# Attention scores as three products of split queries and keys, the parts made per head on ScalarE and GpSimd

## The reference, cut to what matters

```python
q = (x @ wq + bq).reshape(N, H, Dh) * Dh ** (-0.5)      # H = 4 heads, Dh = 128
k = (x @ wk + bk).reshape(N, H, Dh)
v = (x @ wv + bv).reshape(N, H, Dh)
scores = jnp.einsum('ehd,ehd->eh', q[src], k[dst])
smax = jax.ops.segment_max(scores, src, num_segments=N)
ex = jnp.exp(scores - smax[src])
denom = jax.ops.segment_sum(ex, src, num_segments=N)
attn = ex / denom[src]
out = jax.ops.segment_sum(attn[:, :, None] * v[dst], src, num_segments=N)
return out.reshape(N, D) @ wo + bo
```

## Time and profile before

| what | value |
|---|---|
| median of 3 runs | 1652.49 us (1652.28 to 1654.07) |
| the profiled execution, own time | 1657.46 us |
| its span | 1655.8 us |
| TensorE busy | 95% |
| VectorE, ScalarE, GpSimd busy | 71%, 66%, 41% |
| mean granted TensorE clock | 0.989 |
| attention stages of the four blocks | about 234 to 297, 395 to 459, 556 to 620, 715 to 777 us |

### The profile page before, as it was taken

One profiled execution on the slowest core, in us unless ns is written; L12 is line 12 of the kernel. 1 busy time (PEld: TensorE's weight loads), 2 busy tenths in 40 slices (PEclk: granted clock), 3 DMA queues, 4 the chain that ended last, 5 costly groups with the idle time before them and its releaser, 6 DMA issues. The chain is left out here.

```text
span 1655.8 us, 24985 instructions
## 1 busy us (share of the span) xinstructions
PE 1568.6 (95%) x8530; PEld 1222.1 (74%) x8530; DVE 1181.7 (71%) x1900; ACT 1099.5 (66%) x1530; POOL 672.1 (41%) x494
## 2 busy tenths in 40 slices
PE   5789899999999999999999999999999999999987
PEld 5765586878688768877854777777777777777874
DVE  8977645555565546464623499888888888888967
ACT  9841545544554456444530599999999999999962
POOL 3410200120012001200302788888888888888500
PEclk9999899999999999999999999999999999999989
DMA  3001220022012200211106867777777777777710
GB/s 105 0 19 66 90 83 26 20 63 84 26 33 83 77 1 33 83 33 69 49 1 221 162 140 151 149 139 156 141 153 147 149 148 146 150 139 155 163 38 32
DMA packets 107046, 153.94 MB, mean 93 GB/s; under 512 B 42042, under 2 KB 47034, under 8 KB 106466
## 3 DMA queue, kind: packets, MB, share of 16 engines
q0 software_dynamic: 72832, 87.84, 27.3%
q1 hardware_dynamic: 34146, 65.21, 12.2%
HBM read 141.02 MB, written 11.73 MB: 92 GB/s over the span
## 5 line engine op out<-in xcount | busy, mean ns | idle before, releaser
L1752 POOL DMA_INDIRECT edge_gathered<-dst_table,edge_index x158 | 262.2, 1660 | 58.6 <-issue 54.0
L223 PE MATMUL edge_z2p<-edge_w_hi,edge_h_hi 128*128 128x512 f32 x628 | 256.7, 409 | 1.7 <-DVE edge_late L2067 1.7
L223 PE MATMUL edge_z2p<-edge_w_hi,edge_h_lo 128*128 128x512 f32 x628 | 248.7, 396 | 0.0
L223 PE MATMUL edge_z2p<-edge_w_lo,edge_h_hi 128*128 128x512 f32 x628 | 248.5, 396 | 0.0
L1721 POOL DMA_INDIRECT edge_gathered<-src_table,edge_index x158 | 186.3, 1179 | 85.4 <-issue 34.6
L961 POOL TENSOR_TENSOR h<-h,tr_row_b 128x512 f32<-128x512 f32 x40 | 59.1, 1514 | 264.7 <-ACT C L1196 264.4
L950 POOL TENSOR_TENSOR tr_cw<-w_c,tr_cw 32x1024 fp32r<-32x1024 f32 x7 | 16.6, 2375 | 363.7 <-ACT tr_cw L1156 363.7
L223 PEld LDWEIGHTS edge_z2p<-edge_w_hi,edge_h_hi 128*128 128x128 f32 x628 | 118.0, 188 | 54.8 <-issue 29.8
L223 PEld LDWEIGHTS edge_z2p<-edge_w_hi,edge_h_lo 128*128 128x128 f32 x628 | 118.2, 188 | 28.6
L2067 DVE TENSOR_TENSOR edge_late<-edge_z2p,w_c 128x1024 f32<-128x1024 f32 x79 | 96.7, 1224 | 57.3 <-PE edge_z2p L223 55.9
L223 PEld LDWEIGHTS edge_z2p<-edge_w_lo,edge_h_hi 128*128 128x128 f32 x628 | 118.3, 188 | 24.6
(11 more groups left out here) (362 smaller groups left out, 4004.7 us busy)
## 6 DMA issues: line engine op xcount, KB each, us to landing
w_c<-in_attr_T SPq DMA_DIRECT2D x78, 128.0 KB
agg<-edge_sum_rows POOLq DMA_DIRECT2D x36, 128.0 KB
w_a<-in_wv SPq DMA_DIRECT2D x4, 1024.0 KB, 5.4
w_b<-in_wq SPq DMA_DIRECT2D x4, 1024.0 KB, 5.4
w_a<-in_wk SPq DMA_DIRECT2D x4, 1024.0 KB, 7.9
w_b<-in_wo SPq DMA_DIRECT2D x4, 1024.0 KB, 7.0
w_a<-in_m SPq DMA_DIRECT2D x4, 1024.0 KB, 5.3
w_b<-in_m SPq DMA_DIRECT2D x4, 1024.0 KB, 5.4
```

What stands on the lines that cost most here:

```text
L223: mm = pe.matmul(out, a, b, start=(n == 0), stop=(n == last))
L1752: pool.indirect_dma_start(out=from_rows[ring][:, j, :].bitcast(F32), out_offset=None, in_=k.dst_table, in_offset=bass.IndirectOffsetOnAxis ...
```

## The change

The scores become three products like the others. For each head ScalarE copies k (`k_high`) and q (`q_high`) into fp32r high parts, GpSimd subtracts to make the low parts (`low_rows`), and TensorE waits for both (`qk_split`) before a head's first score product. Two k buffers alternate: head 0 and 2 in the first 640 columns of the flattened `hid` buffers, head 1 and 3 in the last chunk of `yT`. The q parts go by node tiles of 128 columns into a ring of 7 slots behind the first k buffer; where five tiles wrap around the ring's end, the copy and the subtraction come in two runs (heads 1 and 2). `k_high(0)` and `q_high(0)` stand ahead of the loop over n, `k_high(h+1)` at n = 5h+1 and `q_high(h+1)` at n = 5h+3 ahead of that n's exponential.

```diff
--- before.py
+++ after.py
@@ -750,6 +750,21 @@
         r, y = k.h, k.C
         yT_hi, yT_lo = sb("yT_hi", [P, KF, NP], F32R), sb("yT_lo", [P, KF, NP], F32R)
         hid_hi, hid_lo = sb("hid_hi", [P, KF, 3 * P], F32R), sb("hid_lo", [P, KF, 3 * P], F32R)
+        flat_hi, flat_lo = (t[:, :, :].rearrange("p c n -> p (c n)") for t in (hid_hi, hid_lo))
+        k_parts = [(flat_hi[:, 0:NP], flat_lo[:, 0:NP]), (yT_hi[:, KF - 1, :], yT_lo[:, KF - 1, :])]
+        Q_RING = 7
+        q_parts = [(flat_hi[:, NP + a * P:NP + (a + 1) * P], flat_lo[:, NP + a * P:NP + (a + 1) * P]) for a in range(Q_RING)]
+
+        def q_runs(h):
+
+            runs, i = [], 0
+            while i < NT:
+                slot = (h * NT + i) % Q_RING
+                n = min(NT - i, Q_RING - slot)
+                runs.append((i, slot, n))
+                i += n
+            return runs
+
         qT, kT, v = sb("qT", [P, KF, NP]), sb("kT", [P, KF, NP]), sb("v", [P, NT, D])
         probs_more = sb("probs_more", [P, NP])
         scores, probs = [k.hT[:, a, :] for a in range(2)], [k.hT[:, 2, :], k.hT[:, 3, :], probs_more[:, :]]
@@ -772,6 +787,7 @@
             sem(n) for n in ("vec", "sca", "var_ready", "rstd_ready", "h_ready", "exp_ready", "probs_ready",
                              "y_ready", "bias_added", "x_joined"))
         y_high, o_high, hidden_split = sem("y_high"), sem("o_high"), sem("hidden_split")
+        qk_high, qk_split = sem("qk_high"), sem("qk_split")
         cb_scaled, cw_high, cw_ready = sem("cb_scaled"), sem("cw_high"), sem("cw_ready")
         gcn_h_ready, edge_h_ready = sem("gcn_h_ready"), sem("edge_h_ready")
         plan = Plan(sem("product_ready"), {"vec": sem("taken_vec"), "sca": sem("taken_sca"), "low": sem("taken_low"),
@@ -951,6 +967,17 @@
                                        ALU.subtract).then_inc(cw_ready, 1)
                     pool.wait_ge(cw_ready, b * 2 + (s + 1))
 
+                def low_rows(b, h):
+
+                    pool.wait_ge(qk_high, (b * HEADS + h) * 2 + 1)
+                    hi, lo = k_parts[h % 2]
+                    pool.tensor_tensor(lo, kT[:, h, :], hi.bitcast(F32), ALU.subtract).then_inc(qk_split, 1)
+                    pool.wait_ge(qk_high, (b * HEADS + h) * 2 + 2)
+                    for i, slot, n in q_runs(h):
+                        at = slice(NP + slot * P, NP + (slot + n) * P)
+                        ins = pool.tensor_tensor(flat_lo[:, at], qT[:, h, i * P:(i + n) * P], flat_hi[:, at].bitcast(F32), ALU.subtract)
+                    ins.then_inc(qk_split, 1)
+
                 pool.wait_ge(cw_ready, 1)
                 cut(0, 1)
                 for b in range(BLOCKS):
@@ -959,9 +986,15 @@
                         pool.wait_ge(y_ready, of_norm(b, s, NT - 1))
                         for i in range(NT):
                             pool.tensor_tensor(r[:, i, :], r[:, i, :], row_b[:, :], ALU.add).then_inc(bias_added, 1)
+                        if s == 0:
+                            for h in range(HEADS - 1):
+                                low_rows(b, h)
+                            pool.wait_ge(qk_split, (b * HEADS + HEADS - 2) * 2 + 2)
                         if b < LAST:
                             pool.wait_ge(bias_added, of_norm(b, s, NT - 1))
                             cut(b + 1, s)
+                        if s == 0:
+                            low_rows(b, HEADS - 1)
                 for i in range(NT):
                     pool.wait_ge(bias_added, of_norm(LAST, 1, i))
                     pool.tensor_tensor(k.x[:, i, :], k.x[:, i, :], r[:, i, :], ALU.add).then_inc(x_joined, 1)
@@ -1050,11 +1083,11 @@
                             h, i = divmod(n, NT)
                             bank = plan.open(pe, ("S", b, n))
                             if i == 0:
-                                plan.need(pe, ("q", b, h, 1))
-                                plan.need(pe, ("k", b, h, 1))
+                                pe.wait_ge(qk_split, (b * HEADS + h) * 2 + 2)
+                            k_hi, k_lo = k_parts[h % 2]
                             for f in range(2):
-                                mm = pe.matmul(bank[:, f, 0:HALF], qT[:, h, i * P:(i + 1) * P],
-                                               kT[:, h, f * HALF:(f + 1) * HALF], start=True, stop=True)
+                                half = slice(f * HALF, (f + 1) * HALF)
+                                mm = three(bank[:, f, 0:HALF], [(q_parts[n % Q_RING], (k_hi[:, half], k_lo[:, half]))])
                             plan.made(mm)
                         if 2 <= n < N + 2:
                             bank = plan.open(pe, ("T", b, n - 2))
@@ -1236,7 +1269,24 @@
                             if f == 0:
                                 high_piece("wk", m)
                     high("wo", b)
+
+                    def q_high(h):
+                        plan.need(act, ("q", b, h, 1))
+                        for i, slot, n in q_runs(h):
+                            ins = act.activation(flat_hi[:, NP + slot * P:NP + (slot + n) * P], qT[:, h, i * P:(i + n) * P], ACT.Copy)
+                        ins.then_inc(qk_high, 1)
+
+                    def k_high(h):
+                        plan.need(act, ("k", b, h, 1))
+                        act.activation(k_parts[h % 2][0], kT[:, h, :], ACT.Copy).then_inc(qk_high, 1)
+
+                    k_high(0)
+                    q_high(0)
                     for n in range(N + 4):
+                        if n % NT == 1 and n < N - NT:
+                            k_high(n // NT + 1)
+                        if n % NT == 3 and n < N - NT:
+                            q_high(n // NT + 1)
                         if n == 4:
                             plan.take(act, ("k", b, KF - 1, 1))
                             loaded_weights("m1", b)
```

## The result

The median of eight runs is 1658.14 us (1657.04 to 1659.37) against 1653.18 us of before, a ratio of 1.0031 (95% interval 1.0022 to 1.004). The change makes the kernel 5 us slower: forecast were 3.0, range and direction hold, and the size is short by 2 us. The range, 1648.0 to 1662.5, was wide enough to hold a gain of 4.5 us as well as a loss of 10, and slower had a chance of only 0.43; what tests the forecast are its single steps.

What follows compares the result with a forecast made beforehand. The bound was taken as the TensorE-VectorE round trip: two tiles take 3.96 us against TensorE's own 3.24. Per block 1.45 + 0.2 - 0.66 - 0.22, about +0.8 (+0.6 last), +3.0 on 1652.49: 1655.5 us, range 1648.0 to 1662.5.

Steps and rivals of the forecast that it cites:

- What TensorE saves: Score products 0.22 us shorter, 17.4 in all; on the path per block only -0.66 in head 2, -0.22 at tile 19.
- the sum for free parts: All attention stages: parts cost nothing, the TensorE-VectorE loop stands; -2.1 us a block, -8.6 in all; its rival's chance 0.15.
- The start: First score product of a stage waits for head 0's parts: 0.75 us late, first transposes +0.5.
- Head 0: Tiles 0 to 4: GpSimd's parts for head 1 make its first score product 1.3 or 1.4 late; +0.5 us more.
- Tiles 5 to 8: ScalarE and VectorE full with m1 splits; k low part of head 2 charged 0.4 us; +0.5 more before first o.
- Rival (2): GpSimd parts queue between VectorE's scalings and splits, up to 1.3 us each: +2.5 a block, +10, 1662.5 us; chance 0.15.
- Head 1: From the first o on: shorter score products -0.4, k parts of head 3 +0.6, net +0.2 us; last block 0.
- The loop's -0.4: Head 1: shorter score products at tile 9 and in the TensorE-VectorE round trip save 0.4 us a block.
- what was charged at +0.6: Head 1, three blocks: head 3's k copy and low part follow cw ops, holding a second scaling (tile 11): +0.6 us.
- The sum: All stage terms together: about +0.8 us a block, +0.6 in the last, +3.0 in all, giving 1655.5 us.
- the rule weighed in the prediction: VectorE op in two-port mode or with two SBUF inputs and GpSimd op exclude each other throughout; collision 0.91 us, not 0.65.
- The 4 us more: Four collisions on the path per block, priced by the full-exclusion rule, would raise the sum by 4 us.

Runs made afterwards that it cites:

- e1: Kernel before with three-product score products on already split yT rows, no copies or low parts (scores wrong): 1645.43 us, ratio 0.995 to before.
- e5: The change with head 0's q parts made ahead of its k parts: 1655.26 us, ratio 1.0019 to the kernel before.
- e6: The change with head 1's k and q parts made ahead of the loop, q in a free yT row: 1655.73 us, ratio 1.0016 to before.
- e8: The change without GpSimd's k low part of head 2, one op less per block: 1653.5 us, ratio 1.0011 to before.
- e3: The change with float32 score products and old waits, without GpSimd's low parts, so only ScalarE's copies added: 1653.46 us, ratio 1.0005 to before.
- e4: The change with k copies of heads 2 and 3 moved under an o product (n = 8 and 13): 1650.21 us, ratio 0.9986 to before.
- e7: The change with head 0's q parts first, head 1's parts before the loop, later k copies under an o: 1647.45 us, ratio 0.997 to before.
- e2: The change with float32 score products; copies and low parts made, but TensorE waits for them only once per block: 1660.26 us, ratio 1.0043 to before.

## Why the prediction was right, and where its sum was short

- **What TensorE saves.** Right. Forecast 3.74 us for two tiles, measured 3.76; head 2 gives -0.60 (forecast -0.66), S(19) -0.21 (-0.22). e1 gives -7.3 to -8, where the sum for free parts was -8.6.
- **The start.** Right in place and size: S(0) 0.67 late (0.75), T(0) 0.55 (0.4 to 0.5). e5 shows it by itself.
- **Head 0.** Right: S(5) waits for GpSimd, 1.18 late (1.3 or 1.4); the scaling of tile 1 took 0.92 for 0.61. GpSimd's 128x640 op takes 1.54 to 1.57 there (1.57), and the q part of head 1 in its two runs 1.97 (1.85). T(3) is 0.95 late (1.0). e6 shows what the place costs, 0.8 us.
- **Tiles 5 to 8.** The term that was mis-sized. "The k low part meets VectorE's split or scaling, and I charge 0.4": it measured 1.36 on the scaling of tile 5, and 1.24 on the first o in e8. The part came just as VectorE turned to the scaling and held it for nearly its own length; I had taken something below the one collision in the earlier trace rows, where GpSimd's op was more than half over when the scaling began. With 1.36 in that place the sum is 0.8 + 0.96 = 1.8 a block, of which head 1 (below) takes 0.26 back, so 1.5 against 1.42 measured. Rival (2), collisions in full, had that op right but not the longer parts.
- **Head 1.** Forecast +0.2, measured -0.06. The loop's -0.4 was right (-0.39 in e1); what was charged at +0.6 measured +0.33. The k copy behind the cw copy, part of that charge, costs nothing in e3, and in three blocks the two collisions behind the cw op cost little more than the one of before. That the q part of head 3 costs nothing under an o was right: its collision, at 427.60 above, is hidden. In the last block I took less than in the others, and it was more, +0.38 measured: without the cw op the k low part of head 3 finds a scaling of its own (1.79 us), and the fourth o is 1.90 late instead of 1.42. e4, which moves that part, gains 2.5 us there and 1.6 to 1.8 in the others.
- **The sum.** +0.8 a block forecast, +1.42 measured, +1.9 in the last: 6.2 against 3.0 by the traces, 5.0 by the medians.

A held scaling ends 0.35 or 0.36 us after the end of the GpSimd row, which is its own 0.61 less 0.25 (399.00 and 399.36; 408.71 and 409.07; in e7 393.06 and 393.42; before, 424.13 and 424.48). All 23 scalings of the change that last over 0.68 do so, as against 3 before, and so do all those of the experiments. In these rows, then, the GpSimd op holds the scaling until 0.25 us before the end of its own row. The price of a collision is set by where in the GpSimd op the scaling begins, from nothing to 1.36 for an op of 1.54; 0.65 was one draw of it and no typical value. So the rule weighed in the prediction, from the Trainium skill, "SBUF — State Buffer", section "Who interferes with whom", holds here but for these 0.25 us. Whether the scaling runs in the mode that the rule asks for no row shows. The 4 us more that the prediction worked out by it would have come nearer to the 6.2 of the sums, but by luck: they were four steps from 0.65 to 0.91, and what the sum lacked was one collision, that of tile 5, which cost more than either.

Left open: no kernel put the low parts on VectorE or split them smaller, and whether the 0.58 at T(0) in e7 can be moved away wasn't tried. That GpSimd's op holds the scaling is shown by e8, where the op is gone and the scaling is back at 0.61; by what means it holds it no run here shows.

## What to carry to other kernels

Where engines follow each other in a loop, price a saving by the round trip of one unit, not by the engine's busy time: less than half of TensorE's saving was on the path here, 7.9 of 17.4 us in e1. GpSimd work that nobody waits for is not free while VectorE scales or splits in SBUF: find the stretch in which nobody waits for VectorE's result either (here under each o product) and put it there. The parts, their copies and the waits for them cost 13.5 us at their first places (+6.2 against -7.3 in e1, by the sums) and 2.3 in e7. And where a wait needs two things, make the one that is ready first ahead of the other: that swap alone gave over 0.7 us a stage.

## What the runs showed of the hardware

A copy into fp32r, or a low part, costs what its columns say: ScalarE takes 0.72 to 0.74 us for 128x640, GpSimd 0.73 for 256 columns (e2), 1.00 for 384 and 1.54 to 1.57 for 640, about 2.1 ns a column more, where VectorE doesn't hold it up. Where VectorE does, its 640 columns take longer: 1.70 behind the cw op in the change, 1.87 in e6. Unexpected was who loses. The scaling of 407.10 starts in the rows before the GpSimd op of 407.17, and yet it is the scaling that waits, for 1.36 us, in all four blocks. In e6, where the scaling starts 0.14 before GpSimd's op and not 0.07, it is GpSimd that waits. The start of a row alone does not tell which of two such ops holds the other up.
